# A vision tower's mixture-of-experts layers: down projection by features, gates applied before it

## The reference, cut to what matters

```python
# M0: 8 experts, hidden 512, top 1;  M2: 8 experts + 1 shared, hidden 384, top 2
y = sum(c[:, e] * ((silu(x @ w1[e]) * (x @ w2[e])) @ w3[e]) for e in experts)   # c: 0 where not chosen
# M3: 16 experts, 8 of hidden 128 and 8 of hidden 256, top 8, no second factor
y = sum(c[:, e] * (gelu(x @ w1[e]) @ w2[e]) for e in experts)
h = h + y          # in M0: bfloat16(y) * max(probs)
```

## Time and profile before

| what | value |
|---|---|
| median of three runs | 915.31 us |
| the profiled execution | 910.74 us, its span 909.0 us |
| TensorE busy, matmul / weight load | 821.0 us (90%) / 722.9 us (80%) |
| VectorE, ScalarE, GpSimd busy | 565.1 (62%), 314.4 (35%), 148.4 us (16%) |
| chain that ended last | TensorE 76%, VectorE 16%, GpSimd 3% |
| mean granted TensorE clock | 0.856 |
| weight loads of these stages, issue to landing | 3.3 to 6.2 us |
| one `drain` (three instructions of L1118 in the timeline) | 1.06 us |
| one `centre` (L1069 to L1071 in the timeline) | 1.1 us |

### The profile page before, as it was taken

One profiled execution on the slowest core, in us unless ns is written; L12 is line 12 of the kernel. 1 busy time (PEld: TensorE's weight loads), 2 busy tenths in 40 slices (PEclk: granted clock), 3 DMA queues, 4 the chain that ended last, 5 costly groups with the idle time before them and its releaser, 6 DMA issues.

```text
span 909.0 us, 16458 instructions
## 1 busy us (share of the span) xinstructions
PE 821.0 (90%) x6576; PEld 722.9 (80%) x6576; DVE 565.1 (62%) x1380; ACT 314.4 (35%) x673; POOL 148.4 (16%) x99
## 2 busy tenths in 40 slices
PE   6899979999998859989896999699999989869998
PEld 5689769999998317768784688589999966758998
DVE  2544368888776445456735166478888866668764
ACT  0333253322221111447721233242323216554452
POOL 1100112221110111123302000211212120022120
PEclk9865559999999555989976999879999979969999
DMA  9700022222330000000200000013131200011200
GB/s 249 224 2 1 1 64 65 64 65 78 95 88 5 1 0 0 1 3 2 68 13 1 1 1 3 2 50 94 48 97 48 82 0 2 3 40 41 83 1 21
DMA packets 16060, 38.80 MB, mean 43 GB/s; under 512 B 3436, under 2 KB 4428, under 8 KB 15598
## 3 DMA queue, kind: packets, MB, share of 16 engines
q1 hardware_dynamic: 14152, 36.71, 14.6%
q10 hardware_dynamic: 1832, 1.04, 0.5%
HBM read 37.27 MB, written 0.44 MB: 41 GB/s over the span
## 4 chain that ended last, share of the span: by engine, by line
PE 76%; DVE 16%; POOL 3%; issue 2%; ACT 2%; DMA 1%; SPq 0%; DVEq 0%
PE PS L538 7%; PE PS L454 7%; PE PS L453 7%; PE PS L452 6%; PE PS L427 5%; PE PS L557 4%; PE PS L591 4%; PE PS L431 4%; PE PS L428 4%; PE PS L430 4%; PE PS L429 4%; PE PS L493 3%; PE PS L646 3%; PE PS L527 3%; DVE XN L919 2%; POOL ssq L1422 2%
## 5 line engine op out<-in xcount | busy, mean ns | idle before, releaser
L454 PE MATMUL PS<-DH,AL 128*96 128x192 f32 x498 | 147.8, 297 | 0.0
L453 PE MATMUL PS<-DL,AH 128*96 128x192 f32 x498 | 147.1, 295 | 0.0
L452 PE MATMUL PS<-DH,AH 128*96 128x192 f32 x498 | 141.0, 283 | 1.9 <-DVE H L1118 1.9
L1090 DVE TENSOR_TENSOR AL<-MIX,AH 128x288 fp32r<-128x288 f32 x166 | 111.0, 669 | 32.2 <-ACT AH L736 27.8
L731 ACT ACTIVATE MIX<-PS 128x288 f32<-128x288 f32 x118 | 48.6, 412 | 209.0 <-PE PS L431 209.0
L452 PEld LDWEIGHTS PS<-DH,AH 128*96 128x96 f32 x498 | 108.2, 217 | 2.3 <-issue 2.3
L454 PEld LDWEIGHTS PS<-DH,AL 128*96 128x96 f32 x498 | 109.8, 221 | 0.0
L453 PEld LDWEIGHTS PS<-DL,AH 128*96 128x96 f32 x498 | 108.4, 218 | 0.0
L427 PE MATMUL PS<-XH,WH 128*128 128x288 f32 x284 | 91.9, 324 | 18.1 <-DVE XL L989 15.0
L428 PE MATMUL PS<-XL,WH 128*128 128x288 f32 x284 | 86.5, 305 | 0.0
L431 PE MATMUL PS<-X,WL 128*128 128x288 f32 x284 | 86.3, 304 | 0.0
(11 more groups left out here) (180 smaller groups left out, 1533.1 us busy)
## 6 DMA issues: line engine op xcount, KB each, us to landing
RG<-in_gu_l0f_dram SPq DMA_DIRECT2D x8, 512.0 KB, 4.4
RG<-in_gu_l0f_dram SPq DMA_DIRECT2D x16, 256.0 KB, 5.6
RG<-in_gu_l2f_dram SPq DMA_DIRECT2D x9, 384.0 KB, 3.3
RG<-in_gu_l2f_dram SPq DMA_DIRECT2D x18, 192.0 KB, 4.1
RD<-in_wd_l0f_dram SPq DMA_DIRECT2D x8, 384.0 KB, 6.2
RD<-in_wd_l2f_dram SPq DMA_DIRECT2D x9, 288.0 KB, 4.6
RD<-in_wd_l3f_dram SPq DMA_DIRECT2D x6, 384.0 KB, 3.9
BIG<-in_patch_dram SPq DMA_DIRECT2D x6, 288.0 KB, 7.9
```

Source lines behind the costliest of these rows:

```text
L452: mm(YB(g), hi, DH[n % RING][:, w], start=first, stop=False, skip_group_check=True)
L453: mm(YB(g), hi, DL[n % RING][:, w], start=False, stop=False, skip_group_check=True)
L454: last = mm(YB(g), lo, DH[n % RING][:, w], start=False, stop=m.last(s, ch), skip_group_check=True)
L1090: V.tensor_tensor(AL[U % 3][:, :], AF[U % 2][:, :], AH[U % 3][:, :].bitcast(F32), ALU.subtract).then_inc(S["ah_lo"], 1)
```

## The change

1. The down projection is turned round. The weights are stationary (128x128 blocks), the 288 activations of the unit move, the result has features on the partitions: banks `FB(j, 0)` (features 0 to 127) and `FB(j, 1)` (the last 64, high and low parts of the weights in one stationary block, rows 0-63 and 64-127). Five matmuls for a unit in place of nine. All experts are summed in these four banks; `drain` is gone.
2. Because the sum is over all experts, the gate is multiplied into the activations before. The router's `c` is split (`CB2`), transposed (`turn_weights`, round 8), and each expert's row is spread over 128 partitions by one matmul for each half, 16 in M0 and M2 (rounds 9 to 12, `spread_both`, two experts a round, copied to SBUF by ScalarE for one half and by VectorE for the other) and 32 in M3 (`spread_run`, left in PSUM). GpSimd multiplies in M0 and M2 (the shared expert of M2, now the first slot, goes without), VectorE in M3 (`weigh`).
3. `down` trails `hidden` by 12 units in M0 and M2, by 20 in M3 (`lag`), in place of 2. The activations wait in twelve or 24 buffers in `OT` and `BIG`. Within a slot the units now run first over the chunks of one half, then over those of the other (`unit`).
4. At the end of a stage ScalarE copies the four banks (`f_sb`), TensorE turns them back to tokens (`by_tokens`; the second block's two halves are added by a matmul), and `stream` adds them to `H`.
5. ScalarE rounds to `AH` (`high`) in all stages. All low parts of weights are now VectorE's: `up_low` twice and `down_low` once per slot. `up_low` for slot `s+1` stands in the 5th and 6th unit of slot `s`. `down_high` and `down_low` trail with the lag.
6. The first slot of each stage is split during the attention stage before (`a.then`). The start of a stage is reordered: `split_x` directly from PSUM, the router's matmuls in rounds 0 and 2, its VectorE work in rounds 3, 4 and 5, `centre` in rounds 16, 20, ... 60.

The core of the diff:

```diff
 # TensorE
-                    for tau in range(TAU):
-                        g = TAU * j + tau
-                        w = slice(ch * C, (ch + 1) * C)
-                        first = m.first(s, ch) and tau != 1
-                        hi, lo = AH[U % 3][:, tau:HN:TAU], AL[U % 3][:, tau:HN:TAU]
-                        mm(YB(g), hi, DH[n % RING][:, w], start=first, stop=False, skip_group_check=True)
-                        mm(YB(g), hi, DL[n % RING][:, w], start=False, stop=False, skip_group_check=True)
-                        last = mm(YB(g), lo, DH[n % RING][:, w], start=False, stop=m.last(s, ch), skip_group_check=True)
+                    W, hi, lo = DW[s % RING][:, ch], AH[U % 3][:, :], AL[U % 3][:, :]
+                    both = W[:, 128:256]
+                    mm(FB(j, 0), W[:, 0:128], hi, start=first, stop=False)
+                    mm(FB(j, 0), W[:, 256:384], hi, start=False, stop=False)
+                    mm(FB(j, 1), both, hi, start=first, stop=False)
+                    mm(FB(j, 0), W[:, 0:128], lo, start=False, stop=final)
+                    mm(FB(j, 1), both, lo, start=False, stop=final).then_inc(S["w3_done"], 1)
...
                 turn(stage, 0, True)
+                for u in range(m.units + m.lag):
+                    if u < m.units:
+                        hidden(u)              # ch == 0 and j == 0: waits for gu_lo of its slot, both parts
+                    if u == 0:
+                        router(*ROUTER[m.name], stage, 0)
                     if u == 1:
                         turn(stage, 1, True)
+                    if u == 2:
                         router(*ROUTER[m.name], stage, 1)
+                    if u == 8:
+                        turn_weights()
+                    if m.up and 9 <= u < 13:
+                        spread_both(2 * (u - 9))       # e >= 1 waits for cb_sb of e - 1, both halves
+                        spread_both(2 * (u - 9) + 1)
+                    if not m.up and 0 <= u - m.lag + 4 < m.units and m.starts_run(u - m.lag + 4):
+                        spread_run(u - m.lag + 4)
+                    if u >= m.lag:
+                        down(u - m.lag)
+                    if u == m.units + m.lag - m.chunks + 1:
+                        by_tokens(0)
+                by_tokens(1)
 # ScalarE: gate(u); u == 0: evac_split(1); u == 3: router_exp; up_high in units 4 and 5 of a slot;
 #          u == 8: weights_turned; spread copies; high(u - lag + 2); down_high
 # VectorE
+                for u in range(m.units + m.lag):
+                    if m.up and u < m.units:
+                        product(u)
+                    if u == 0:
+                        split_x(m, 1)
+                    if u == 3:
+                        view = router_shift(m)
+                    if u == 4:
+                        router_mask(m, view)
+                    if u == 5:
+                        router_weights(m, i, view)
+                    if m.up and 9 <= u < 13:
+                        spread(2 * (u - 9))
+                        spread(2 * (u - 9) + 1)
+                    if not m.up and 0 <= u - m.lag + 3 < m.units:
+                        weigh(u - m.lag + 3)
+                    if 0 <= u - m.lag + 1 < m.units:
+                        low(u - m.lag + 1)
+                    s, v = u // m.per, u % m.per
+                    if s + 1 < m.slots and 4 <= v < 6:
+                        up_low(m, s + 1, v - 4)
+                    s, v = (u - m.lag) // m.per + 1, (u - m.lag) % m.per
+                    if u >= m.lag and v == 2 and s < m.slots:
+                        down_low(m, s)
+                    if m is M0 and u >= 16 and u % 4 == 0 and u // 4 - 4 < NC_ * A1.ng:
+                        centre(u // 4 - 4)
 # GpSimd, M0 and M2
+                        pool.wait_ge(S["a_ready"], u0 + u + 1)
+                        pool.wait_ge(cb_sb[j], 8 * mi + e + 1)
+                        G.tensor_tensor(af(arg, u), af(arg, u), weight(arg, e, j), ALU.mult).then_inc(S["am_ready"], 1)
```

More of the change, by code:

```diff
@@ L105 @@
 SG0 = {M0.name: 0, M2.name: M0.units}
[L106 to L110, removed]
+AM0 = {m.name: sum(x.weighted(u) for x in MOES[:i] for u in range(x.units)) for i, m in enumerate(MOES)}
+SLOTS = [(m, s) for m in MOES for s in range(m.slots)]
 RING = 2
@@ new lines, in spread_both, with spread_run @@
+                def spread_both(e):
+                    if e == 0:
+                        pe.wait_ge(S["ct_sb"], mi + 1)
+                    for j in range(2):
+                        if e >= 1:
+                            pe.wait_ge(cb_sb[j], 8 * mi + e)
+                        spread(e, j, 6 + j)
+                def spread_run(u):
+                    x = m.run(u)
+                    if x == 0:
+                        pe.wait_ge(S["ct_sb"], mi + 1)
+                    if x >= 2:
+                        pe.wait_ge(S["am_ready"], max(mixed(m, v) for v in range(m.units) if m.run(v) == x - 2))
+                    spread(m.expert(u), m.unit(u)[1], 2 + x % 2)
@@ L455, in down @@
-                    last.then_inc(S["w3_done"], 1)
-                turn(stage, 0, True)
-                for u in range(m.units + 2):
+                    if m.up and s == 0 and ch == 0:
+                        for i in range(2 if j else 0):
+                            pe.wait_ge(cb_sb[i], 8 * (mi + 1))
+                    W, hi, lo = DW[s % RING][:, ch], AH[U % 3][:, :], AL[U % 3][:, :]
+                    first, final = s == 0 and ch == 0, s == m.slots - 1 and ch == m.chunks - 1
+                    both = W[:, 128:256]
@@ L727, in moe, with gate @@
+            def moe(m, k):
+                u0, mi = MU0[m.name], MOES.index(m)
+                def gate(u):
+                    U = u0 + u
                     act.wait_ge(S["g_ready"], U + 1)
@@ L744, in router_exp @@
+                for j in range(2):
+                    act.wait_ge(S["w3_done"], u0 + m.units - (1 - j) * m.chunks)
+                    for part in range(2):
+                        activation(summed(m, j, part), FB(j, part), ACT.Copy).then_inc(S["f_sb"], 1)
             def router_exp(i, w, rows):
@@ L1275, in attention @@
                         norm(i - lag - 2)
+                    if a.then and 5 <= i < 7:
+                        up_low(a.then, 0, i - 5)
+                    if a.then and i == 7:
+                        down_low(a.then, 0)
             def grid_attention():
```

525 lines of the change are left out of this document (295 added, 230 removed).

## The result

The changed kernel took 927.74 us in the median of four executions (917.54 to 929.7), the kernel before 913.98 us beside it: ratio 1.014, interval 1.010 to 1.018. Executions more than 1.5% above the fastest of their kernel are left out of those two ratios; with all of them in, the medians are 917.31 against 914.29 us and 920.96 against 913.69. So I had forecast 903, about 1% faster, and what came is no gain, or a loss of 1%.

A forecast was written before the change was run, and what follows sets the result against it. TensorE, never without work inside the expert stages, was taken as the bound, at 0.132 us per matmul start. Savings led by -87.6 and added costs summed to -9.0 from 910.7, giving 902; predicted 903 us, range 868 to 936.

The forecast's parts named there:

- the price of the move: Three attention stages: copies moved there, some 3 us on ScalarE and as much on VectorE, cost +3 us, between 0 and 9.
- Matmuls added: Expert stages: 64 matmuls to spread the gates cost +8.4 us, about 25 small ones per stage +3.
- Stage starts: Start of each expert stage: first matmul comes 2.8 us earlier in M0, 4.3 in M2, 2.4 in M3, -9.5.
- Clock at the starts: Starts of the expert stages: more pauses cost +4 us through the clock; 9 us at half speed cost 4.3.
- Router: First rounds of the expert stages: TensorE waits for router work, +9 us in M2, +3 in M0, +2 in M3.
- Spreading: Rounds 9 to 12: the second expert's matmuls wait 1.4 us for copies each round, +7 us in M0, +6.7 in M2.
- VectorE and GpSimd in M0: M0's steady part: three heavy rounds per slot and waits for GpSimd cost TensorE +10 us, 5 to 17.
- M2's borders: Before each further slot's first `hidden` in M2: TensorE idles 2.05 to 2.8 us waiting for `up_low`, +17.5 us.
- The clock at the borders: Seven slot borders of M2: the clock falls at one or two, +6 us, between 0 and 30.
- slow rival: M2's borders: clock falls after pauses above 2 us, 4.3 us each, all seven possible; 934 us, chance 0.21.
- M3 without `down`, ends: M3: rounds without `down` run at 0.8 us a unit, the last 20 at 0.83, +4; stage ends +4.5.
- The whole saving arrives: Expert stages: the long lag hides all waits but the start's, some 55 us less than before, 855 us; chance 0.1.

The follow-up runs named there:

- e13: Changed kernel with M3's first weights split later in A3 (high parts two rounds later, low parts after VectorE's last softmax): 901.52 us, ratio 0.987.
- e1: Changed kernel run again, unedited: ratio 1.0002 to the kernel before, longer executions left out.
- e18: The kernel of e13 run again: ratio 0.994 to the kernel before over the shorter executions.
- e16: Changed kernel run once more, unedited: ratio 1.0007 to the kernel before, longer executions left out.
- e12: Kernel before with 20 spare matmuls, fifteen before A3's turn and five after: ratio 1.0004 over shorter executions, median of all 934.1 us.
- e3: Changed kernel with twelve spare matmuls before the wait for low weights at M2's borders, from the third slot on: 922.91 us.
- e5: Changed kernel with M3's first weights split at M3's start again, not inside A3: 927.93 us, ratio 1.019.
- e8: Changed kernel with the edits of e2 (in all three expert stages), e5, e6 and e7 together: 885.17 us, ratio 0.972.
- e10: The kernel of e9 with M3's first weights also split later in A3: 904.67 us, ratio 0.992.
- e17: The kernel of e5 run again: one execution at 904.2 us, three at 926 to 930.
- e6: Changed kernel with VectorE's block copy and 128-column transposes back in the turn, replacing the extra matmuls: 920.0 us, ratio 1.010.
- e14: The kernel of e11 without any spare matmul: 853.11 us, ratio 0.934.
- e7: Changed kernel with the first expert's gates spread ahead of `hidden` and the second's after it, rounds 9 to 12: 924.14 us, ratio 1.013.
- e2: Changed kernel with the next slot's up weights rounded and their low parts made two rounds earlier in M2: 885.21 us, ratio 0.972.
- e4: Changed kernel with GpSimd multiplying only 8 of 288 columns in M0 and M2, waits kept: 888.33 us, ratio 0.977.
- e11: Changed kernel with the edits of e2 in all stages, e6, e9 and e10: 858.83 us, ratio 0.939.
- e9: Changed kernel with 17 spare matmuls in TensorE's pauses between M2's last down matmul and A3's projection: 912.33 us, ratio 1.0005.
- e15: The kernel of e11 with 12 more spare matmuls before A3's second turn: 859.96 us, ratio 0.941.

## Why the prediction was wrong

Its sum was -9.0 us from the profiled execution. By stage its terms are: M0 -10.7, M2 +12.3, M3 -13.7, attention +3. The traces have (before against the changed kernel, and in brackets e13): M0 -6.7 (-8.3; e1 -8.1), M2 +13.8 (+13.8), M3 -9.8 (-10.9), A3 +9.8 (+0.7), the other attention stages -2.4 (-2.6), the lead +1.9 (-2.0).

**The step that failed is the price of the move**, +3 with an upper end of 9. I counted the durations of the copies on both engines and took a part as being on the path. What the move costs is not duration: two copies of 0.6 and 0.7 us make two pauses 0.5 and 0.7 longer, and after the second TensorE is at half clock for 54 us. In A3 alone that is 9.1 us (67.8 against 58.7 in e13). I had priced clock falls for the starts and for M2's borders, and never asked it of the attention stages, whose matmuls I had not changed.

With the copies later (e13) the time is 901.5 at a ratio of 0.987, which is the forecast (903 over 915.3 is 0.987). That agreement is in part luck: M0, M2 and M3 together gave -5.4 where -12.1 was forecast, and that is made up by the lead (-2.0, where the sum had nothing) and the attention stages (-1.9, where it had +3). e18, the same kernel, has 0.994.

**The other part is the executions in which the clock does not come back, more frequent after the change and not explained.** Executions with A3 at half throughout cost 16 us over the others of the changed kernel: 12 of 25 are in the longer group, against 13 of 76 above 930 us of the kernel before. For the changed kernel the traces of e16 and e1 show it in A3 (83.6 against 67.8); of the kernel before no long execution was traced, so that its are of this kind is inferred: they lie some 24 us above its others, A3 at 83.6 in place of 58 would be 25.6, and e12's long trace has A3 at 77. What decides whether the clock comes back in the projection stays open: the traces of e3, e5 to e8, e10, e16 and e17 have A3 at 83.5 to 83.9, the others not; e13 had no long execution in four, e18, the same kernel, five in ten. It was three of four in the result, which is why that ratio is 1.014 and the later ones are 1.000. The two parts make up the miss: 903, 6 to 7 more for the move and 16 for the long executions are about 926, against 927.74.

**Step by step.**
- *Down projection*, -87.6: right, five matmuls 0.13 apart.
- *Matmuls added*, +3 for the small ones: the turn's halves cost 1.9 us a turn, of which M0 shows 2.8 and M3 3.5 in e6: some 6 us in place of under 1.
- *Stage starts*, -9.5: from the last matmul of the attention to the first `hidden` it takes 6.3, 7.7 and 6.9 us before and 4.5, 4.6 and 4.6 after, -7.2 in sum; the turn's halves stand in it (e6: 1.1 less in M0 and M3).
- *Clock at the starts*, +4: M3 begins at half clock for 31 us after (816 to 847) and for 27 in e13, before for 17 (801.5 to 818.5). The 14 and 10 us more are worth up to 7 and 5; M3 falls short of its forecast by 3.9 and 2.8. e14, with the shorter turn and the earlier weights, has it at 92.0.
- *Router*, M2 +9: 9.86 us of idle where 11 was forecast. M0: 5.0 in two pauses in the first trace and 6.2 in e1, against 5.5. M3: 1.9 before `hidden`, but released by ScalarE's `OT` and not by the wait for slot 1, which is 0.4.
- *Spreading*, 1.4 for each of eight rounds: half right. Two rounds of four in M0 and two in M2 wait 1.3 to 1.5, the others 0.3 to 0.5. It costs 4.0 in M0 and some 3.5 in M2 beside the matmuls, against 7 and 6.7. Dividing it gave nothing (e7); in e2, where ScalarE's weight copies stand in earlier rounds, the waits of 1.27 in M2 are 0.54.
- *VectorE and GpSimd in M0*, +10 (5 to 17): the pauses before `down` are 6.1 us (the group of L543 above), and e4 shortens M0 by 7.4. The instruction that waits for GpSimd was the wrong one: I had named `AL`, with a mean well over 0.7 us as the sign. It is 0.47 in M0 and 0.46 in M2, against 0.63 and 0.84 before the change; `up_low` is the one that waits, 1.6 us in M0 and 1.4 in M2.
- *M2's borders*, +17.5: six pauses of 2.39 and one of 1.78 make 16.1. Right, and for the reason given. The Trainium skill's figure for GpSimd ("GPSIMD Engine Reference", 3.1 Elementwise, about twice as slow as VectorE on two inputs, an estimated 0.9 us) was nearer than my 0.75: 0.93 in M2, 0.94 to 1.03 in M0.
- *The clock at the borders*, +6 for one or two falls: five falls in e1 (four in the first trace) at 1.4 us each, 6.9 by e3. The size came out by luck, from two wrong factors. The slow rival put each at 4.3 and would have been right in kind and far off in price, since after a border the clock is back in 3.4 us (6.8 at the first one in some traces) and not in 9. Its point of 2 us does not hold either: the first trace has a fall after the pause of 1.78 and after three of the six of 2.39, and one in A3 after 1.44.
- *M3 without `down`, ends*: TensorE is busy throughout the middle of M3, as before, and the last rounds come 0.80 us apart, against 0.83. What the rounds without `down` cost cannot be told: they are the ones at half clock.

**The rival that lives.** The slow one said that clock falls decide. They do, but in A3, where I had not looked. "The whole saving arrives" was called least likely (855 us, 0.1), and e14 reaches 853 with another order in the queues and the turn of before: its condition, that `hidden` be decoupled from VectorE's low parts, is what two rounds earlier give.

## What to carry to other kernels

When an engine is relieved, place the short instructions on which its next block waits (here the next weights' low parts) well ahead of the border, where nothing else stands in front of them: 27 us of 172 in M2. When work is moved to "idle" time of another stage, look at whose queue it enters, what TensorE waits for behind it, and what the clock does after that pause: here the copies made two pauses 0.5 and 0.7 us longer, and A3 took 9 us more. Compare kernels by stages of the trace when whole executions come in two groups.

## What the runs showed of the hardware

- The clock came back 3.4 to 6.8 us after it fell at a border of M2 in the changed kernel (10.2 once, in e6), and 3 to 27 us after falls in the start of M3 (e11, e13); in A3 it stayed at half for 83 us with TensorE busy 97% of the time (e5).
- No single length of pause parts the falls from the rest: it fell after 1.44 us in A3 and after 1.78 in M2, and did not fall after three of six pauses of 2.39 in M2 (first trace) or after the six of 1.6 in e4.
- Spare matmuls in the pauses at A3's entry put the fall off (7 us later in e9, 10 in e12, than in the same kernels without them); in e15 A3 had none, and M3's start was at half for 20 us in place of 14 (e14).
- After the change GpSimd's 128x288 product takes 0.93 to 1.03 us, and 8 columns of it still 0.33 to 0.48 (e4). A VectorE instruction with both inputs in SBUF that starts 0.2 us after it, with 0.75 of it left, takes 0.6 longer (0.96 becomes 1.54 to 1.57); one that starts 0.16 before it takes its usual 0.45.
